# Reading a table into TensorE's and ScalarE's registers with and without a check of the values' bounds

## The reference

```python
x = x + xattn(layernorm(x), ctx, ctx, Wq, Wk, Wv, Wfc, bfc)     # 32 heads, 8 groups of keys and values
x = x + ffn(layernorm(x), ...)
# ffn, for n = 1024 tokens, E = 64 experts with hidden width 64, the best 4 of each token:
logits = flat @ Wr.T + 0.5 * dom                 # dom: a small softmax over 4 domains, by batch
topk_idx = top_k(logits + router_bias, 4)
combine = softmax weights of the four, normalised, 0 elsewhere
h = silu(flat @ Wg[e]) * (flat @ Wu[e]) * combine[:, e]
out = sum over e of h @ Wd[e]  +  sum over 2 shared experts of (silu(flat @ Sg) * (flat @ Su)) @ Sd
```

## Time and profile before

| | |
|---|---|
| median of 3 runs | 387.12 us |
| the 3 runs | 388.15, 381.62, 387.12 us |
| the profiled execution's own time | 383.25 us |
| its span, first to last instruction | 381.4 us |
| PE busy | 268.0 us, 70% of the span |
| DVE, ACT, POOL busy | 202.8, 153.1, 129.6 us |

### The profile page before, as it was taken

One profiled execution on the slowest core, in us unless ns is written; L12 is line 12 of the kernel. 1 busy time (PEld: TensorE's weight loads), 2 busy tenths in 40 slices (PEclk: granted clock), 3 DMA queues, 4 the chain that ended last, 5 costly groups with the idle time before them and its releaser, 6 DMA issues.

```text
span 381.4 us, 6106 instructions
## 1 busy us (share of the span) xinstructions
PE 268.0 (70%) x1726; PEld 193.7 (51%) x1726; DVE 202.8 (53%) x546; ACT 153.1 (40%) x454; POOL 129.6 (34%) x219
## 2 busy tenths in 40 slices
PE   4689999999988993499500000099999998897710
PEld 3465676677745882388400000067777776575400
DVE  5587778787665731138481000036566664565762
ACT  2358787777764432000400000054444664443300
POOL 4246032212220177301777777000000014445371
PEclk9789999999999999569855555579999999898955
DMA  7720066335643599980225333035555556576461
GB/s 211 205 83 2 1 223 214 131 132 188 165 112 80 142 220 328 317 182 14 97 110 165 107 99 110 28 98 169 166 168 169 171 179 187 171 209 212 130 178 57
DMA packets 60000, 56.54 MB, mean 148 GB/s; under 512 B 5116, under 2 KB 56896, under 8 KB 59968
## 3 DMA queue, kind: packets, MB, share of 16 engines
q1 hardware_dynamic: 55360, 43.57, 39.6%
q0 software_dynamic: 4608, 12.59, 11.0%
HBM read 34.12 MB, written 22.02 MB: 147 GB/s over the span
## 4 chain that ended last, share of the span: by engine, by line
PE 49%; issue 25%; SPq 9%; DVE 6%; DMA 4%; ACT 3%; POOL 1%; another core or an unknown queue 1%; POOLq 0%; ACTq 0%; DVEq 0%
PE bank L1532 10%; PE bank L1554 10%; PE bank L1158 9%; SPq L417 5%; PE bank L1309 4%; PE bank L1299 4%; PE bank L1319 4%; PE bank L1162 3%; SPq L414 3%; DMA before_wlo<-in_L_xattn_Wfc 2%; PE bank L1452 2%; POOL after_whi L579 1%; PE bank L1470 1%; DVE mx L796 1%
## 5 line engine op out<-in xcount | busy, mean ns | idle before, releaser
L1158 PE MATMUL bank<-ident,xt_all 128*128 128x128 f32 x128 | 26.5, 292 | 60.1 <-issue 60.1
L579 POOL DMA_INDIRECT after_whi<-y_slots,idx x32 | 31.3, 978 | 102.5 <-DMA y_slots<-after_wlo 88.2
L723 ACT ACTIVATE after_wlo<-bank 128x256 f32<-128x256 f32 x64 | 24.5, 383 | 94.1 <-PE bank L1158 89.0
L1113 DVE TENSOR_TENSOR after_wlo<-bank,after_wlo 128x128 f32<-128x128 f32 x64 | 18.7, 292 | 79.8 <-ACT after_wlo L728 70.7
L1158 PEld LDWEIGHTS bank<-ident,xt_all 128*128 128x128 f32 x128 | 24.8, 197 | 64.6 <-issue 61.8
L796 DVE TENSOR_REDUCE mx<-bank 128x4 f32<-128x512 f32 x64 | 41.8, 685 | 13.3 <-PE bank L1299 12.5
L1532 PE MATMUL bank<-w_all,after_wlo 128*64 128x128 f32 (+1 forms) x384 | 44.4, 298 | 4.3 <-ACT after_wlo L723 4.0
L624 ACT ACTIVATE before_w<-bank 128x512 f32<-128x512 f32 x64 | 38.1, 613 | 17.4 <-PE bank L1309 17.4
L563 POOL DMA_INDIRECT x_slots<-x_all,idx x28 | 27.2, 972 | 30.6 <-DVE idx L921 22.3
L1532 PEld LDWEIGHTS bank<-w_all,after_wlo 128*64 128x64 f32 x384 | 28.2, 143 | 16.0 <-issue 15.3
L1126 DVE COPY after_wlo<-bank 128x256 f32<-128x256 f32 x64 | 27.1, 423 | 7.7 <-remote 2.5
(11 more groups left out here) (212 smaller groups left out, 589.6 us busy)
## 6 DMA issues: line engine op xcount, KB each, us to landing
x_slots<-before_sil SPq DMA_DIRECT2D x8, 1024.0 KB, 6.0
xt_all<-x_slots SPq DMA_DIRECT2D x64, 128.0 KB
y_slots<-after_wlo SPq DMA_DIRECT2D x64, 128.0 KB
w_all<-in_L_ffn_Wg SPq DMA_DIRECT2D x8, 512.0 KB, 3.9
w_all<-in_L_ffn_Wu SPq DMA_DIRECT2D x8, 512.0 KB, 5.6
w_all<-in_L_ffn_Wd SPq DMA_DIRECT2D x16, 256.0 KB, 6.1
out<-xb_all SPq DMA_DIRECT2D x8, 128.0 KB
x_all<-in_x SPq DMA_DIRECT2D x1, 896.0 KB, 5.3
```

Source lines behind the costliest of these rows:

```text
L579: nc.gpsimd.indirect_dma_start(out=got[b % 3][:, k * D:(k + 1) * D], out_offset=None, in_=y_slots[0:last * P], in_offset=bass.IndirectOffs ...
L723: nc.scalar.activation(xTs[g % 2], XT_ps[g % 2][:, 0:D], copy).then_inc(a_xs, 1)
L1158: return nc.tensor.transpose(out_, in_, ident[0:k, 0:k])
```

## The change

```diff
@@ ScalarE's program, line 746
             at = nc.values_load_multi_w_load_instructions(
-                erow[0:1, DYNAMIC:2 * DYNAMIC], engines=[mybir.EngineType.Activation], min_val=0, max_val=(E - 1) * GU)[1]
+                erow[0:1, DYNAMIC:2 * DYNAMIC], engines=[mybir.EngineType.Activation], min_val=0, max_val=(E - 1) * GU,
+                skip_runtime_bounds_check_because="the table is a bitwise and with the number of experts less one, times a constant")[1]
@@ TensorE's program, line 1558
             at = nc.values_load_multi_w_load_instructions(
-                erow[0:1, 0:DYNAMIC], engines=[mybir.EngineType.PE], min_val=0, max_val=(E - 1) * GU)[1]
+                erow[0:1, 0:DYNAMIC], engines=[mybir.EngineType.PE], min_val=0, max_val=(E - 1) * GU,
+                skip_runtime_bounds_check_because="the table is a bitwise and with the number of experts less one, times a constant")[1]
```

## The result

Before: 384.38 us median of 20 runs (379.95 to 388.80). After: 379.58 us median of 20 runs (375.16 to 386.13). The ratio is 0.987, with a 95% interval of 0.983 to 0.991: some 5 us faster, inside the 2% that I had called no change. I had forecast 359. The profiled execution of after took 380.1 us (span 378.3), that of before 383.25 (span 381.4). The ratios here compare only the faster executions of the two kernels, so they can differ a little from the ratio of the medians, and e3 and e5 had too few for one.

A forecast was written before the change was run, and what follows sets the result against it. PE's idle gap from 202.79 to 247.69 us, filled by slowed register checks, was taken as the bound. 383.25 - 44.9 + 19 = 357.4 us, forecast as 359 for the median, range 338 to 382.

The forecast's parts named there:

- The checks fill the gap, and their slowness comes from outside: PE's gap, 202.79 to 247.69 us: checks slowed beside POOL's gathers; all 32 pairs at the early pace would take 9.0 us.
- The loads stay, 2.5 us, and the start is bound by the last scatter: Register loads on PE and ACT remain; PE then waits for the first tile's load, bound by POOL's last scatter, landed 202.79.
- Removed: 44.9 us: With 64 check instructions gone from each engine, PE's tile loop starts at 202.8 instead of 247.7, 44.9 us less.
- The overlap costs 19 us, by 0.43 us for each us of gathers: 29 down gathers beside the loop's start slow it: 36.7 us at 0.43 is 15.6, taken as 19; other end 44.
- second rival: Checks only sat in a gap something else makes; the loop creeps until 240 to 247, 373 to 386 us; chance 0.24.
- forecast's own range: Total of 348 to 372 us, for overlap costs of 8 to 32 us; chance 0.45.
- First rival: Down gathers beside the tile loop cost little, 0 to 5 us, total 340 to 345 us; chance 0.27.
- Third rival: POOL's gathers stretch from 1.254 to 1.6 us and the loop stands until then: slower, 396 us; chance 0.04.
- The net gain: Whole kernel: 44.9 us removed against 19 us of overlap, 383.25 to 357.4 us on the profiled execution.

The follow-up runs named there:

- e3: Kernel after, each gather of down weights waits for the landing of the one before, one in flight: 377.64 us (370.07 to 378.83).
- e5: Kernel after, gather j of down weights waits until DVE has done the hidden rows of j + 1 tiles: 347.52 us (338.35 to 353.29).
- e2: Kernel before, checks kept, without POOL's 32 gathers of down weights: 342.13 us, ratio 0.890.
- e1: Kernel after without POOL's 32 gathers of down weights, tiles 32 to 63 using the down matrices of tiles 0 to 31: 334.54 us, ratio 0.873.
- e6: Kernel after, down gathers issued in pairs, POOL waiting for the landing of each second one: 353.19 us, ratio 0.933.
- e10: Kernel after, the 32 down gathers replaced by plain transfers of the same bytes from a fixed place, issued by GpSimd: 342.61 us, ratio 0.885.
- e7: Kernel after, the same 32 gathers with 256 bytes a row in place of 1,024: 379.83 us, ratio 0.990.
- e11: Kernel before, with its checks, gather j of down weights waiting until tile j's product of gate and up stands: 353.41 us, ratio 0.909.
- e12: Kernel after, gather j of down weights waiting until tile j's product stands, in more rounds: 350.69 us, ratio 0.905.
- e13: Kernel after, two small GpSimd memsets, each waited for, behind each down gather: 318.16 us, ratio 1.002, in a set where the kernel before took 316.74.
- e15: Kernel before, with its checks, two small GpSimd memsets behind each down gather: 316.59 us, ratio 0.997, in a set where the kernel before took 316.74.
- e14: Kernel after, five small GpSimd memsets behind each down gather: 322.75 us, ratio 1.013, in a set where the kernel before took 316.74.

## Why the prediction was wrong

*The checks fill the gap, and their slowness comes from outside.* Right: e2 has the same 64 instructions at a median of 146 and 18 ns once the gathers are gone. A few are still slow (up to 0.70 us) with the last scatters beside them, so all 32 pairs take 13.3 us and not 9.0.

*The loads stay, 2.5 us, and the start is bound by the last scatter.* Right: 2.555 us, and PE starts at 206.45, the forecast 202.8 and the 3.64 us that were lost earlier. The Trainium skill gives 200 ns for each register ("Runtime: NRT & Kernel Launch", Instruction fetch mechanics); the same page describes these loads as loads from HBM, and `erow` lies in SBUF. No run here has 200 ns: 32 registers in one instruction take 2.23 to 2.62 us, 0.07 to 0.08 each.

*Removed: 44.9 us.* Right as the time at which PE starts, wrong as a gain.

*The overlap costs 19 us, by 0.43 us for each us of gathers.* **This is the step that failed.** In the runs the first result of after is out 49.7 us behind its last scatter (251.69 less 202.0), that of e1, without gathers, 11.9 us. The overlap costs 37.8 us at the first result, about one us for each us of gathers. With the measured term the sum is 383.25 - 44.9 + 37.8 + 3.7 = 379.9, against 380.1 of the profiled execution. That it closes says only that no other term of size is missing, as the 37.8 come from the same trace. The cost had both ends in the text, 15.6 and 44, and I took a value near the wrong one. Rows 8 had given a loss averaged over bursts of four with pauses of 2.5 to 4.2 us between them, in which the loop catches up at 0.91 us a tile. A rate from such a stretch holds for bursts with pauses. It was a little low besides, since I took 1.55 us a tile as the undisturbed pace throughout, and from tile 48 or so the loop runs at 1.43 where nothing holds it. e6 and e5 show the effect of the shape outright: a pair holds the loop for 0.3 to 1.0 us, three for about 2, both mostly made good, and 29 in a row stop the loop. The row with the right shape was the crawl of the checks itself, the only one beside an unbroken run of gathers: the same engines, the same transfers, a slowdown of ten. I had written it down, as what speaks for the second rival, and then sized the cost from the other.

One reading beside it was loose too. I called what DVE waits for in the earlier trace rows a product of ACT. The same instruction also waits for PE's product of the up weights, done earlier, and in the stop it is PE's signals that are late, so this row doesn't show a late signal of ACT.

The measured 379.58 lies inside the 338 to 382 that I gave, but only because that range took in most of the second rival. The forecast's own range ended at 372, so this is no credit to the forecast.

*First rival, no cost of overlap, 340 to 345.* Wrong where the stop was there. The numbers of e1 and e10 (334.5 and 342.6) show what it would have looked like. The Trainium skill's rule behind it ("SBUF — State Buffer", SBUF: two separate sides), that transfers and engines cannot slow each other at their ports, may hold as it stands: e7 with a quarter of the bytes has the whole stop, and e10 with all of them has none. So what holds the engines here is not the amount of data at the memory ports, and the rule doesn't protect them from it.

*Second rival, the checks only sat in a gap that something else makes, 373 to 386.* This is what happened, at 379.6: PE and ACT get one or two steps of the loop done and stand, and of its "3 to 6 tiles, or none" it was none. The size of a single hold was other than it had: waits of 4.7 to 22 us for PE's signals, not 1.4 us for each instruction. I gave it 0.24.

*Third rival, POOL's pace stretches.* It did not: 0.95 and 0.30 us all through, as before.

*The net gain.* It is what the loop and the checks got done in the crawl: 7.3 us behind POOL's last gather. Where nothing crawls the checks' 9 to 13 us lie beside the last scatter, its landing and the load of the first tile: 4 to 5 us show (e1 against e2, e11 against e12), or none (e13 against e15).

*What stays open.* That the indirect form is needed, that a quarter of the bytes does the same, and that one transfer at a time does no harm is shown. What delays PE's signals inside the chip, and whether the slow register instructions of PE and ACT have the same cause, is not. Whether two must be in flight, or GpSimd must issue without a pause, is not: e13 and e14 were to tell and ran where there was no stop. Nor is it known what differed in that set. The kernels, the data and the index of the chip were the same as in sets with the stop, and nothing that runs on one core's trace shows what else the chip did. That something outside the kernel takes part is shown; what it is was not tried.

## What to carry to other kernels

When a stretch of register instructions is slow, ask first at what pace the same instructions run elsewhere in the trace. If that is several times faster, removing them may only give the gap to whatever slows them, and the next work in line stands in their place, as it did here. Take the price of an overlap from a row of the same shape (unbroken against bursts), not from the nearest row of the same loop. And where GpSimd's indirect transfers aren't needed at once, don't issue them in one run: a gather for each tile took 9.5% off (e12), and 9.1% with the checks kept (e11), where the change by itself took 1.3%. Spacing them by two memsets lost nothing where there was no stop (e15, e13); by five it lost 1.3% (e14). Whether such spacing removes the stop no run shows.

## What the runs showed of the hardware that I had not expected

- Beside an unbroken run of indirect transfers of GpSimd (128 rows each, one every 1.25 us) TensorE's signals arrive late. An engine that waits for one stands 4.7 to 6.3 us, and once 22, though the product had been done for 7 to 33 us. Signals of ScalarE and VectorE pass in 0.04 to 0.06 us in the same stretch. Register instructions of TensorE and ScalarE take 0.70 us in place of 0.018 or 0.146. VectorE's and GpSimd's own work keeps its pace.
- The same number of bytes in plain transfers of GpSimd's queue, one every 0.6 us with 4.5 us to landing, does not do it; a quarter of the bytes in indirect ones does.
- With one indirect transfer at a time (3.6 us apart) the loop keeps its 1.55 us a tile.
- The effect was absent in one set of seven, on a chip of the same index as one that had shown it before: the kernel before took 316.7 us in place of 384, with the same wait (DVE's for `erow`) at 0.99 us in place of 4.86.
- A check of a register costs 0.28 us of its engine's instruction queue (146 and 18 ns and what lies between them); 32 of them are 9.1 us where none is slow (e15).
